# The second norm's normalised rows move from ScalarE to VectorE

## The chip, the cores and the metric

The kernel runs on one core of a Trainium2 chip. The metric is the device time of one launch in microseconds. Five engines work side by side, each through its own queue in program order: TensorE (PE in the profile), VectorE (DVE), ScalarE (ACT), GpSimd (POOL) and SyncE (SP), which issues most transfers. They wait for each other through semaphores.

## The reference

Two sequences of 1024 tokens, each of width 256, go through one adaptive-norm transformer block:

```python
h = _layernorm(x) * (1 + ca) + sa            # norm 1, modulated
# attention branch, applied to h:
x_norm = (h - mu) / sqrt(var + EPS) * gamma + beta   # norm 2
q, k, v = x_norm @ qkv ...; causal softmax; out @ o_proj; + h
x = x + ga * attention(h)
h = _layernorm(x) * (1 + cb) + sb            # norm 3
# 16 experts, top 4 of each token, and a shared expert
x = x + gb * ffn(h)
```

`sa, ca, ga, sb, cb, gb` come from a small matrix product of `silu(c)` and are the same for all tokens of a sequence. The change is inside norm 2: the rows `xn = (h - mean) / sqrt(var + EPS)` of a tile of 128 tokens, before `gamma` and `beta`.

## The kernel before

The 2048 tokens are 16 tiles of 128. The first part of the kernel, to about 160 us, is one software pipeline over steps `s` from -5 to 17. In a step every engine does a piece for several tiles, each at another stage. The order of work is written out by hand, engine by engine, in one loop per engine; nothing reorders it, so an instruction that waits holds everything behind it on its engine.

The path of tile `t` through the part that matters here:

- Step `t-5` and `t-4`, VectorE: statistics of `x_in` (L1043, L1050), `h = (x_in - mean) * (1 + ca)` (L1377). GpSimd makes `rstd = (var + EPS)^-0.5` (L594, L598). VectorE finishes `h` with `rstd` and `sa` (L1388) and takes the statistics of `h` (L1043, L1050).
- Step `t-3`, GpSimd: `inverse_std` makes norm 2's `rstd` (one operation for up to three norms of different tiles, from step 2 on), `mean_shift` makes `shift = -mean * rstd` (L604), `residual` adds the skip connection to `x1` (L613, L616). From step 9 on four scattered row transfers (L631) follow in each step.
- Step `t-3`, ScalarE: `xn = rstd * h + shift` (L868), near the end of the step.
- Step `t-2`, TensorE transposes `xn` (L1759). ScalarE applies `gamma` and `beta` and makes the high part of a split (L833, L839), VectorE the low part (L1055). Products are made as three products of high and low parts (L1540 to L1542).
- Step `t-1`, TensorE makes value and query rows (`vq`), ScalarE copies the high part (L857), VectorE the low part (L1060). Step `t`: scores, row maximum (L1356), exponential (L848). Step `t+1`: probabilities transposed (L1718), multiplied with the values, `x1` finished (L1412). Norm 3, the router and the sending of rows to the experts follow.

The start of the pipeline is mixed with preparations. On VectorE, step -3 begins with the split of a weight product (L1006), the gate `ga` of the first sequence (L982 to L991) and a gated weight product (`wvo_gate`, L1015). On TensorE the transposition of tile 0's `xn` stands ahead of the modulation of the second sequence (L1547), the modulation columns (L1599), the second gate (L1547) and the transposition of tile 1. Step 4 ends on VectorE with `wvo_gate` for the second sequence (L1015), which ScalarE splits (L719) at the start of step 5.

After the pipeline GpSimd sends the remaining rows (L631, to about 210 us), and then pairs of tiles of routed rows go through the experts (to about 325 us), and the sums are made and stored.

Of the kernel before, what the change touches and what calls it, by code (L numbers as in the profile page):

```python
# [9 lines left out]
ALU = mybir.AluOpType  # L10
ACT = mybir.ActivationFunctionType
# [9 lines left out]
TILES = B * NT  # L21
# [138 lines left out]
def place_of(n, t):  # L160


    return (t + n - 1) % 4
# [9 lines left out]
def adaln_block(nc, x, qkv, o_proj, gamma, beta, w_router, we1, we3, we2, ws1, ws3, ws2, c_in, wmod, out):  # L173
# [3 lines left out]
    with ctx:  # L177
# [10 lines left out]
        def at(name, where, shape, dt=F32):  # L188
            return nc.alloc_sbuf_tensor_at(name, list(shape), dt, offset=ORIGIN + 4 * where)

        def sb(name, shape, dt=F32):
            n = 1
            for m in shape[1:]:
                n *= m
            where = free[0]
            free[0] += (n + 7) // 8 * 8
            return at(name, where, shape, dt)
# [13 lines left out]
        h = at("h", A + 7680, [P, 2, D])  # L211
        xn = at("xn", A + 8192, [P, 2, D])
# [67 lines left out]
        mv = sb("mv", [P, 3, 4, 2])  # L280
        veps = sb("veps", [P, 3, 4])
        rstd = sb("rstd", [P, 3, 4])
        shift = sb("shift", [P, 3, 4])
# [76 lines left out]
        def pv_side(t, at_, n):  # L360
# [25 lines left out]
        tl = {n: sem("t_" + n) for n in (  # L386
            "bn1", "stat1", "u", "h", "bn2", "stat2", "xlo", "negmax", "vqlo", "ptlo", "rinv", "x1", "bn3", "stat3",
            "hlo",
            "shift2", "shift3", "rmul", "resid", "z2", "h2row", "lg",
            "xT", "vq", "scores", "pT", "h2T", "pv",  # L390
            "xn", "xf", "xhi", "exp", "vqhi", "pthi", "h2f", "hhi")}
# [3 lines left out]
        def inverted(eng, n, t):  # L395

            eng.wait_ge(s_rstd, POWERS[n, t])

        def done(eng, stage_, t):

            if t >= 0:
                eng.wait_ge(tl[stage_], t + 1)
# [143 lines left out]
        def _(pool):  # L546
# [89 lines left out]
            for s in range(FIRST, LAST + 2):  # L636
                if s < 0 <= s + 3:
                    residual(s + 3)
                for group in norms_of(s):
                    inverse_std(group)  # L640
                    for n, t in reversed(group):
                        if n > 1:
                            mean_shift(n, t)
                if 0 <= s and s + 3 < TILES:
                    residual(s + 3)
                if s == 3:
                    router_constants()
                send(SENDS.get(s, 0))
# [22 lines left out]
        def _(act):  # L671
# [8 lines left out]
            def load_table(func):  # L680

                act.wait_ge(s_eps, 1)
                if tables[0]:
# [25 lines left out]
                                 scale=D ** -0.5).then_inc(s_wqk_hi, 1)  # L709
# [82 lines left out]
            for s in range(FIRST, LAST + 1):  # L792

                if s == -2:
                    wvo_copy()
                if s == 1:
                    gate_b_copy()
                if s == 5:
                    wvo_split(1)
                if 0 <= s - 4:  # L800
                    norm2_cols(s - 4)
                if s == LAST:
                    norm2(s - 3)
                    norm2_rows(s - 5)
                t = s - 1
                if 0 <= t < TILES:

                    for u, first, n in units_of(t):
                        done(act, "pT", u)
                        if u >= PT_RING:  # L810
                            done(act, "pv", tile_of_unit(u - PT_RING))
                        nc.scalar.activation(pT_hi[:, u % PT_RING, 0:n * P], ps[:, X0 + u % 2, 0:n * P],
                                             ACT.Copy).then_inc(tl["pthi"], 1)
                if s == LAST:
                    router_exp(NG - 2)
                    load_table(ACT.Silu)
                    silu_step(0)
                if 0 <= s - 3 and s < LAST:
                    norm2(s - 3)
                if 0 <= s - 4:  # L820
                    if s - 5 >= 0 and s < LAST:
                        norm2_rows(s - 5)
                    norm2_hi(s - 4)
                t = s + 2
                if 0 <= t < TILES:

                    at = slot_of(t) * P
                    done(act, "xT", t)
                    if t == 0:
                        act.wait_ge(s_ld_cols, 32)  # L830
                    done(act, "xlo", t - 2)
                    for c in range(DC):
                        last = nc.scalar.activation(xf[:, t % 2, c, :], ps[:, Y0, c * P:(c + 1) * P], ACT.Identity,  # L833
                                                    scale=cols[:, 0, c:c + 1], bias=cols[:, 1, c:c + 1])
                    last.then_inc(tl["xf"], 1)
                    done(act, "xf", t)
                    if t >= KEY_SLOTS:
                        done(act, "scores", NT - 1)
                    nc.scalar.activation(xnT_hi[:, :, at:at + P], xf[:, t % 2, :, :], ACT.Copy  # L839
                                         ).then_inc(tl["xhi"], 1)  # L840
                t = s
                if 0 <= t < TILES:

                    done(act, "negmax", t)
                    if t >= 2:
                        done(act, "pT", units_of(t - 2)[-1][0])
                    done(act, "rinv", t - 4)
                    nc.scalar.activation(probs[:, t % 2, 0:(t % NT + 1) * P], score_banks(t), ACT.Exp,  # L848
                                         bias=negmax[:, t % 4:t % 4 + 1],
                                         accum_out=rowsum[:, t % 4:t % 4 + 1]).then_inc(tl["exp"], 1)  # L850
                t = s + 1
                if 0 <= t < TILES:
                    done(act, "vq", t)
                    done(act, "scores", t - 2)
                    if t >= KEY_SLOTS:
                        done(act, "pv", NT - 1)
                    nc.scalar.activation(vq(V_HI, Q_HI, t), ps[:, Y1, :].rearrange("p (two x) -> p two x", two=2),  # L857
                                         ACT.Copy).then_inc(tl["vqhi"], 1)
                if s == -2:
                    wvo_split(0)  # L860
                    gate_a_copy()
                    load_table(ACT.Exp)
                t = s + 3
                if 0 <= t < TILES:

                    done(act, "shift2", t)
                    done(act, "xT", t - 2)
                    nc.scalar.activation(xn[:, t % 2, :], h[:, t % 2, :], ACT.Identity,  # L868
                                         scale=rstd[:, 1, place_of(2, t):place_of(2, t) + 1], bias=shift[:, 1, t % 4:t % 4 + 1]
                                         ).then_inc(tl["xn"], 1)  # L870
                if s - 1 in RANKED_AT and s < LAST:
                    router_exp(RANKED_AT.index(s - 1))
                if 12 <= s < 12 + SH:
                    split_shared(s - 12)
# [78 lines left out]
        def _(dve):  # L953
# [91 lines left out]
            def stats_end(n, t, read_by):  # L1045
                done(dve, f"bn{n}", t)
                done(dve, read_by, t - 4)
                if n == 1 and t >= 4:
                    inverted(dve, n, t - 4)
                nc.vector.bn_aggr(mv[:, n - 1, place_of(n, t), :], bn[:, n - 1, place_of(n, t), :]).then_inc(tl[f"stat{n}"], 1)  # L1050

            def x_lo(t):
                at = slot_of(t) * P
                done(dve, "xhi", t)
                nc.vector.tensor_tensor(xnT_lo[:, :, at:at + P], xf[:, t % 2, :, :],  # L1055
                                        xnT_hi[:, :, at:at + P].bitcast(F32), ALU.subtract).then_inc(tl["xlo"], 1)
# [275 lines left out]
            for s in range(FIRST, LAST + 1):  # L1332
# [11 lines left out]
                t = s - 1  # L1344
# [7 lines left out]
                t = s  # L1352
# [7 lines left out]
                a, c = s + 5, s + 4  # L1360
# [20 lines left out]
                    stats_end(1, a, "u")  # L1381
                if 0 <= s + 2 < TILES and s > -1:
                    x_lo(s + 2)
                if 0 <= c < TILES:

                    inverted(dve, 1, c)
                    done(dve, "u", c)
                    nc.vector.scalar_tensor_tensor(out=h[:, c % 2, :], in0=h[:, c % 2, :],  # L1388
                                                   scalar=rstd[:, 0, c % 4:c % 4 + 1], in1=mod_a[:, c // NT, 0:D],
                                                   op0=ALU.mult, op1=ALU.add).then_inc(tl["h"], 1)  # L1390
                t = s - 1
# [10 lines left out]
                t = s - 1  # L1402
# [10 lines left out]
                                                   scalar=rinv[:, t % 4:t % 4 + 1], in1=x1[:, t, :],  # L1413
                                                   op0=ALU.mult, op1=ALU.add).then_inc(tl["x1"], 1)
                if 0 <= c < TILES:
                    stats_end(2, c, "shift2")
                if 0 <= t < TILES:
                    done(dve, "x1", t)
                    stats(3, x1[:, t, :], t)
# [546 lines left out]
```

## Time and profile before

| | |
|---|---|
| Times of three runs | 377.86, 380.18, 382.19 us |
| Median | 380.18 us |
| Profiled execution, span from first to last instruction | 380.9 us |
| TensorE busy | 329.5 us, 87% of the span |
| VectorE busy | 258.2 us, 68% |
| GpSimd busy | 213.2 us, 56% |
| ScalarE busy | 197.8 us, 52% |
| Mean granted TensorE clock | 0.952 of full |

The profiled execution has no time of its own in the record beside its span of 380.9 us, which is 0.7 us above the median of the three runs. In rows of the timeline the first number is the start in us from the span's start, the second how long the instruction or the merged run of instructions took. Square brackets give the idle time of the engine ahead of the row and who ended it. Instructions of one engine overlap by a little under 0.1 us, so the distance from start to start is shorter than the time of one.

### The profile page before, as it was taken

Reading aid. Unit: us, or ns where it says so; the run is one execution under the profiler, and the core shown is the slowest. Engines: PE = TensorE matmul, PEld = TensorE weight load, DVE = VectorE, ACT = ScalarE, POOL = GpSimd, SP = SyncE. Lnnn points to the kernel's source line nnn. Section 1 sums busy time; section 2 is a strip of 40 time slices with the busy share of each in tenths; the row PEclk is TensorE's granted clock in tenths of the full one; section 3 lists DMA queues with packets and bytes.
Section 4 is the critical chain, followed back from the end, with each engine's and each line's share of the span. In section 5 each row is a group of like instructions: output and inputs, shape, how many; then the busy total and the mean of one; then the engine's idle time right before and its main releaser. Section 6 shows DMA issues by size and latency. Waiting matters only on the chain.

```text
span 380.9 us, 8085 instructions
## 1 busy us (share of the span) xinstructions
PE 329.5 (87%) x2296; PEld 305.0 (80%) x2296; DVE 258.2 (68%) x720; ACT 197.8 (52%) x436; POOL 213.2 (56%) x289
## 2 busy tenths in 40 slices
PE   3986997997888999999890399999999998999890
PEld 1676997997887899898770389999999998988770
DVE  1888895578985886757891379656656555516996
ACT  2456666465675656746340078656666665621100
POOL 1486563333388887757777007766666666651240
PEclk9999897799999999999997589999999999999997
DMA  6346500000011229982232346666675666239952
GB/s 217 115 148 203 166 28 16 8 20 14 3 62 70 79 92 316 305 271 111 108 126 108 95 98 183 186 184 201 174 207 166 197 187 175 91 91 412 409 191 83
DMA packets 54554, 56.36 MB, mean 148 GB/s; under 512 B 17424, under 2 KB 46864, under 8 KB 54512
## 3 DMA queue, kind: packets, MB, share of 16 engines
q1 hardware_dynamic: 46560, 34.21, 30.6%
q0 software_dynamic: 6864, 19.80, 13.7%
q10 hardware_dynamic: 1088, 1.84, 1.4%
q8 instruction: 21, 0.34, 0.4%
q14 instruction: 21, 0.17, 0.2%
HBM read 31.43 MB, written 24.40 MB: 147 GB/s over the span
## 4 chain that ended last, share of the span: by engine, by line
PE 44%; POOL 13%; DVE 11%; DMA 10%; issue 9%; SPq 8%; ACT 3%; DVEq 0%; POOLq 0%; ACTq 0%
PE ps L1540 11%; PE ps L1541 11%; PE ps L1542 11%; POOL xg_rows L631 7%; DMA y_in<-y_rows 4%; SPq L523 3%; PE ps L1863 3%; SPq L518 3%; POOL y_rows L658 2%; DMA x_in<-in_L_attn_x_dram 2%; DMA xs<-xg_rows 2%; PE ps L1694 1%; PE ps L1896 1%; POOL rstd L598 1%; PE ps L1633 1%
## 5 line engine op out<-in xcount | busy, mean ns | idle before, releaser
L658 POOL DMA_INDIRECT y_rows<-y_sb,aside x79 | 76.5, 969 | 53.0 <-ACT y_sb L930 38.9
L631 POOL DMA_INDIRECT xg_rows<-hrow,slot_u x64 | 66.3, 1037 | 20.7 <-issue 18.9
L1540 PE MATMUL ps<-rpool 128*128 128x256 f32 (+3 forms) x228 | 70.8, 311 | 6.3 <-DVE rpool L1060 6.2
L1541 PE MATMUL ps<-rpool 128*128 128x256 f32 (+3 forms) x228 | 67.8, 297 | 0.0
L1542 PE MATMUL ps<-rpool 128*128 128x256 f32 (+3 forms) x228 | 67.7, 297 | 0.0
L1540 PEld LDWEIGHTS ps<-rpool 128*128 128x128 f32 x228 | 45.5, 200 | 8.9 <-DVE rpool L1060 8.3
L1540 PE MATMUL ps<-w_hi_routed,xT_hi 128*128 x158 | 45.8, 290 | 2.2 <-DVE xT_lo L1469 2.1
L1542 PEld LDWEIGHTS ps<-rpool 128*128 128x128 f32 x228 | 45.5, 199 | 0.6
L1541 PEld LDWEIGHTS ps<-rpool 128*128 128x128 f32 x228 | 45.5, 200 | 0.5
L1542 PE MATMUL ps<-w_hi_routed,xT_lo 128*128 x158 | 45.2, 286 | 0.0
L1541 PE MATMUL ps<-w_lo_routed,xT_hi 128*128 x158 | 45.2, 286 | 0.0
L1469 DVE TENSOR_TENSOR xT_lo<-ps,xT_hi 128x512 fp32r<-128x512 f32 x40 | 27.6, 691 | 17.1 <-ACT xT_hi L905 17.1
L1863 PE MATMUL ps<-ident,xs 128*128 128x128 f32 x158 | 25.0, 284 | 15.1 <-DMA xs<-xg_rows 15.1
L594 POOL TENSOR_TENSOR veps<-mv,eps 128x1 f32<-128x1 f32 (+2 forms) x26 | 6.7, 257 | 53.6 <-DVE mv L1050 53.2
L905 ACT ACTIVATE xT_hi<-ps 128x512 fp32r<-128x512 f32 x40 | 24.0, 599 | 21.2 <-PE ps L1863 19.4
L1540 PEld LDWEIGHTS ps<-w_hi_routed,xT_hi 128*128 128x128 f32 x158 | 30.7, 194 | 3.4 <-issue 3.4
L1487 DVE TENSOR_TENSOR aside<-ends,aside 128x2 int32<-128x2 int32 (+1 forms) x40 | 6.5, 162 | 39.4 <-ACT r_silu L921 39.4
L921 ACT ACTIVATE r_silu<-ps 128x256 f32<-128x256 f32 x40 | 15.4, 385 | 33.6 <-PE ps L1542 30.9
L1863 PEld LDWEIGHTS ps<-ident,xs 128*128 128x128 f32 x158 | 19.2, 146 | 15.7 <-DMA xs<-xg_rows 15.7
L1542 PEld LDWEIGHTS ps<-w_hi_routed,xT_lo 128*128 128x128 f32 x158 | 30.8, 195 | 0.0
L1541 PEld LDWEIGHTS ps<-w_lo_routed,xT_hi 128*128 128x128 f32 x158 | 30.8, 195 | 0.0
L1540 PE MATMUL ps<-h2T_hi,w_hi_shared 128*128 128x512 f32 x64 | 26.9, 420 | 0.0
(208 smaller groups left out, 893.4 us busy)
## 6 DMA issues: line engine op xcount, KB each, us to landing
xs<-xg_rows SPq DMA_DIRECT2D x79, 128.0 KB
y_in<-y_rows SPq DMA_DIRECT2D x8, 1024.0 KB, 12.1
xg_rows<-empty SPq DMA_DIRECT2D x1, 2304.0 KB, 8.2
x_in<-in_L_attn_x_dram SPq DMA_DIRECT2D x16, 128.0 KB, 2.1
w_raw_routed<-in_L_ffn_we_dram SPq DMA_DIRECT2D x8, 256.0 KB, 3.8
out_dram<-x SPq DMA_DIRECT2D x16, 128.0 KB, 2.4
wmod_sb<-in_L_wmod_dram ACTq DMA_DIRECT2D x3, 512.0 KB, 7.4
w_raw_routed<-in_L_ffn_we_dram SPq DMA_DIRECT2D x4, 320.0 KB, 7.0
```

The source lines that it names most:

```text
L518: sp.dma_start(xs[:, r, i, :], xg[bass.ds(row[i], P), 0:D]).then_inc(s_xs[r], 16)
L523: sp.dma_start(ends[:, r, i, :], xg[bass.ds(row[i], P), bass.ds(col[i], 2)]).then_inc(s_ends[r], 16)
L594: nc.gpsimd.tensor_tensor(v, mv[:, norms, j, 1], eps[:].broadcast_to(wide), ALU.add).then_inc(s_veps, 1)
L631: nc.gpsimd.indirect_dma_start(out=xg, out_offset=bass.IndirectOffsetOnAxis(ap=slot_u[:, t, k:k + 1].bitcast(U32), axis=0), in_=hrow[:, t, ...
L658: nc.gpsimd.indirect_dma_start(out=yb, out_offset=bass.IndirectOffsetOnAxis(ap=dest[:, 2 * n + i:2 * n + i + 1].bitcast(U32), axis=0), in_ ...
L905: nc.scalar.activation(xT_hi[:, n % 2].rearrange("p i c t -> p (i c t)"), ps[:, 6 + n % 2, :], ACT.Copy).then_inc(s_rxhi, 1)
L921: nc.scalar.activation(r_silu[:, n % 2], ps[:, n % 2, :].rearrange("p (i w) -> p i w", i=2)[:, :, 0:H], ACT.Silu).then_inc(s_rsilu, 1)
L1469: nc.vector.tensor_tensor(xT_lo[:, n % 2].rearrange("p i c t -> p (i c t)"), ps[:, 6 + n % 2, :], xT_hi[:, n % 2].rearrange("p i c t -> p ...
L1540: nc.tensor.matmul(dst, w[0], x_[0], start=first, stop=False)
L1541: nc.tensor.matmul(dst, w[0], x_[1], start=False, stop=False)
L1542: return nc.tensor.matmul(dst, w[1], x_[0], start=False, stop=last)
L1863: last = nc.tensor.transpose(ps[:, 6 + n % 2, (i * DC + c) * P:(i * DC + c + 1) * P], xs[:, n % RING, i, c * P:(c + 1) * P], ident[:])
```

## The change

ScalarE's activation for `xn` and GpSimd's `shift` of norm 2 go. VectorE makes `xn` in one operation, `(h - mean) * rstd`, with mean and `rstd` read per partition. It stands in the step of before (`t-3`), between the low part of tile `s+2` and the second half of `h` of tile `s+4`, and waits for `rstd` of norm 2, for VectorE's own statistics and for the transposition of tile `t-2`. The statistics of `h` four tiles on now wait for `xn`, which is on the same engine. Norm 3 keeps its shift on GpSimd and its activation on ScalarE.

```diff
@@ GpSimd
                     inverse_std(group)
-                    for n, t in reversed(group):
-                        if n > 1:
+                    for n, t in group:
+                        if n == 3:
                             mean_shift(n, t)
@@ ScalarE
-                t = s + 3
-                if 0 <= t < TILES:
-
-                    done(act, "shift2", t)
-                    done(act, "xT", t - 2)
-                    nc.scalar.activation(xn[:, t % 2, :], h[:, t % 2, :], ACT.Identity,
-                                         scale=rstd[:, 1, place_of(2, t):place_of(2, t) + 1], bias=shift[:, 1, t % 4:t % 4 + 1]
-                                         ).then_inc(tl["xn"], 1)
@@ VectorE
                 if 0 <= s + 2 < TILES and s > -1:
                     x_lo(s + 2)
+                t = s + 3
+                if 0 <= t < TILES:
+
+                    j = place_of(2, t)
+                    inverted(dve, 2, t)
+                    done(dve, "stat2", t)
+                    done(dve, "xT", t - 2)
+                    nc.vector.tensor_scalar(xn[:, t % 2, :], h[:, t % 2, :], mv[:, 1, j, 0:1], rstd[:, 1, j:j + 1],
+                                            ALU.subtract, ALU.mult).then_inc(tl["xn"], 1)
                 if 0 <= c < TILES:
@@ VectorE, statistics of h
-                    stats_end(2, c, "shift2")
+                    stats_end(2, c, "xn")
```

Where the new operation falls for tile 0 is seen on VectorE in step -3. Before, the engine's row reads as follows (`gate_tmp` and `mod_a` are the gate, `wT_sb` the gated weight product, `mv` a mean and variance):

```order
L1006 SCALAR_TENSOR_TENSOR rpool<-ps,rpool 128x512
L982 TENSOR_SCALAR gate_tmp<-ps 128x256
L984 COPY mod_a<-ps 128x256
L986 SCALAR_TENSOR_TENSOR mod_a<-mod_a 128x256
L989 TENSOR_SCALAR mod_a<-mod_a 128x256
L991 SCALAR_TENSOR_TENSOR mod_a<-gate_tmp,mod_a 128x256
L1015 TENSOR_TENSOR wT_sb<-wT_sb,mod_a 128x256 x2
L1043 BN_STATS bn<-x_in 128x6
L1377 SCALAR_TENSOR_TENSOR h<-x_in,mv,mod_a 128x256
L1050 BN_AGGR mv<-bn 128x2
L1388 SCALAR_TENSOR_TENSOR h<-h,rstd,mod_a 128x256
```

With the change the same place on VectorE reads (L1383 is the new operation; the other lines are those above, eight lower, and L1389 the old L1388):

```order
L998 SCALAR_TENSOR_TENSOR rpool<-ps,rpool 128x512
L974 TENSOR_SCALAR gate_tmp<-ps 128x256
L976 COPY mod_a<-ps 128x256
L978 SCALAR_TENSOR_TENSOR mod_a<-mod_a 128x256
L981 TENSOR_SCALAR mod_a<-mod_a 128x256
L983 SCALAR_TENSOR_TENSOR mod_a<-gate_tmp,mod_a 128x256
L1007 TENSOR_TENSOR wT_sb<-wT_sb,mod_a 128x256 x2
L1035 BN_STATS bn<-x_in 128x6
L1369 SCALAR_TENSOR_TENSOR h<-x_in,mv,mod_a 128x256
L1042 BN_AGGR mv<-bn 128x2
L1383 TENSOR_SCALAR xn<-h,mv,rstd 128x256
L1389 SCALAR_TENSOR_TENSOR h<-h,rstd,mod_a 128x256
```

Tile 0's `xn` now stands behind the weight split, the gate, the gated weight product and the first half of tile 1's `h`.

On ScalarE it stood ahead of the copy of the weight product (L714), as this piece of the difference shows:

```order
 L704 ACTIVATE wT_sb<-ps 128x512
 L708 ACTIVATE rpool<-ps 128x512
-L868 ACTIVATE xn<-h,shift,rstd 128x256
 L714 ACTIVATE wT_sb<-ps 128x512
 L833 ACTIVATE xf<-ps,cols 128x128 x2
```

Nothing stood ahead of it there but the copies of the weight products, so it ran as soon as `shift` was there. TensorE's order is unchanged.

## Rows read from the trace of the kernel before

**Rows 1.** The page's chain of work that ended last, by engine.

```profile
PE 44%; POOL 13%; DVE 11%; DMA 10%; issue 9%; SPq 8%; ACT 3%; DVEq 0%; POOLq 0%; ACTq 0%
```

**Rows 2.** Windows: stretch, length, then busy time per engine, PEclk, DMA share, GB/s.

```profile
36.00:40.00 4.00, 2.86 (x11) 2.86 (x12) 3.34 (x12) 0.46 (x3) 1.17 (x3) 0.67 0.80 226
40.00:44.00 4.00, 3.68 (x28) 3.44 (x27) 3.21 (x9) 3.29 (x9) 2.09 (x4) 0.90 0.82 235
...
60.00:64.00 4.00, 2.90 (x15) 2.93 (x16) 3.46 (x9) 3.36 (x10) 0.93 (x2) 0.66 0.13 37
64.00:68.00 4.00, 4.00 (x20) 4.00 (x20) 1.03 (x2) 1.08 (x2) 0.00 (x0) 0.50 0.01 2
68.00:72.00 4.00, 4.00 (x21) 3.92 (x20) 2.14 (x8) 1.53 (x4) 0.72 (x2) 0.56 0.00 0
...
120.00:124.00 4.00, 3.38 (x28) 3.31 (x29) 3.84 (x19) 3.40 (x9) 3.45 (x6) 1.00 0.09 36
```

**Rows 3.** Timeline of TensorE, 14 to 38 us.

```profile
14.37 1.89 PE L1578 MATMUL ps<-o_sb,wT_sb 128*128 128x256 f32 x8
16.69 0.44 PE L1759 MATMUL ps<-ident,xn 128*128 128x128 f32 x2 [0.42 <-ACT xn L868]
16.96 2.75 PE L1547 MATMUL ps<-wmod_sb,silu_b 128*128 128x512 f32 x8
...
21.25 1.11 PE L1547 MATMUL ps<-wmod_sb,silu_b 128*128 128x256 f32 x4
23.14 0.44 PE L1759 MATMUL ps<-ident,xn 128*128 128x128 f32 x2 [0.78 <-ACT xn L868]
...
37.14 0.53 PE L1540 MATMUL ps<-rpool 128*128 128x384 f32 x1 [1.60 <-DVE rpool L1060]
```

**Rows 4.** Timeline of VectorE, 18 to 35 us.

```profile
18.88 0.61 DVE L1377 SCALAR_TENSOR_TENSOR h<-x_in,mv,mod_a 128x256 f32<-128x256 f32 x1
19.41 0.17 DVE L1050 BATCH_NORM_AGGREGATE mv<-bn 128x2 f32<-128x6 f32 x1
...
26.85 1.03 DVE L1377 SCALAR_TENSOR_TENSOR h<-x_in,mv,mod_a 128x256 f32<-128x256 f32 x1
...
34.82 0.43 DVE L1043 BATCH_NORM_STATS2 bn<-x_in 128x6 f32<-128x256 f32 x1 [1.51 <-DMA x_in<-in_L_attn_x_dram]
```

**Rows 5.** Instructions of a line: count, then ns shortest/median/longest, first and last start.

```profile
L868 ACT ACTIVATE xn<-h,shift,rstd x16: 589/598/601, 16.0 to 128.7; 128x256 f32<-128x256 f32 x16
...
L604 POOL TENSOR_SCALAR shift<-mv,rstd x32: 261/267/740, 15.7 to 166.3; 128x1 f32<-128x1 f32 x32
...
L989 DVE TENSOR_SCALAR mod_a<-mod_a x2: 293/295/297, 16.5 to 51.1; 128x256 f32<-128x256 f32 x2
...
L1377 DVE SCALAR_TENSOR_TENSOR h<-x_in,mv,mod_a x16: 466/468/1031, 13.0 to 114.2; 128x256 f32<-128x256 f32 x16
...
L1388 DVE SCALAR_TENSOR_TENSOR h<-h,rstd,mod_a x16: 472/482/953, 13.6 to 119.4; 128x256 f32<-128x256 f32 x16
```

**Rows 6.** Groups by line on VectorE, 188 to 193 us: busy us, mean ns.

```profile
L1204 DVE TENSOR_SCALAR tb<-tb,lane 128x16 f32<-128x16 f32 x1 | 0.2, 227 | 0.0
...
L1199 DVE TENSOR_SCALAR tb<-tb 128x16 f32<-128x16 f32 x1 | 0.2, 174 | 0.0
```

**Rows 7.** Timeline of TensorE: the waits in steps 5 and 11.

```profile
61.10 0.54 PE L1759 MATMUL ps<-ident,xn 128*128 128x128 f32 x2 [2.23 <-ACT hrow L790]
...
120.62 0.38 PE L1540 MATMUL ps<-rpool 128*128 128x256 f32 x1 [1.86 <-DVE rpool L1060]
```

**Rows 8.** Timeline of GpSimd, steps 9 to 11.

```profile
101.78 0.51 POOL L604 TENSOR_SCALAR shift<-mv,rstd 128x1 f32<-128x1 f32 x2
...
110.51 0.79 POOL L604 TENSOR_SCALAR shift<-mv,rstd 128x1 f32<-128x1 f32 x2
...
118.49 0.89 POOL L598 TENSOR_TENSOR rstd<-veps,minus_half 128x3 f32<-128x3 f32 x1
```

**Rows 9.** Timeline of VectorE, step 11.

```profile
119.42 0.48 DVE L1388 SCALAR_TENSOR_TENSOR h<-h,rstd,mod_a 128x256 f32<-128x256 f32 x1 [3.34 <-POOL rstd L598]
```

## The prediction

> **What bounds the kernel now.** I read the chain that ended last first: TensorE has 44% of it, GpSimd 13%, VectorE 11%, ScalarE 3% [rows 1]. So the engine that is relieved most carries almost nothing of the end, and ScalarE's 16 activations of 0.598 us, 9.6 us of busy time [rows 5], say little about the time. Then I went through the timelines of the pipeline, since the change lies in it alone, and asked in each step who waits last. From step 12 on TensorE has no idle time worth naming, and the sending of rows and the experts start from its end, so what the steps up to there win or lose moves everything behind them by the same amount. Four places are not TensorE's own: the start up to 44 us, where VectorE, GpSimd and a transfer take turns; step 4 to 5, where TensorE sits idle for 2.23 us behind a chain that starts on VectorE [rows 7]; steps 9 to 11, where GpSimd is full and VectorE waits 3.34 us for its `rstd` [rows 9]; and two spells at half clock. Those show in the windows: from 36 to 44 us the granted clock is 0.67 and 0.90, from 60 to 72 us it is 0.66, 0.50, 0.56 [rows 2]. Lost clock is 4 x (0.33 + 0.10) = 1.7 us in the first and 4 x (0.34 + 0.50 + 0.44) = 5.1 us in the second. Both begin when TensorE comes back from a wait, of 1.60 us [rows 3] and of 2.23 us [rows 7]. A wait of 1.86 us at 120.62 did not lower it: 120 to 124 us is at 1.00 [rows 2, 7].
>
> **The price of the new operation.** No row shows it. Nearest is the one-input operation on 128x256 numbers from SBUF with constants, 0.295 us; from start to start it is some 0.08 less [rows 5]. A scalar read per partition costs 0.227 - 0.174 = 0.05 us in a small operation [rows 6]. With two of them I take 0.40 us, 0.3 from start to start, because shape and memory are those of the first row. The lower bound is 0.22, the upper 0.95 - 0.08 = 0.87, the longest `h` operation beside GpSimd [rows 5]. It comes 16 times, 6.4 us of busy time; what counts is the places where nothing covers it.
>
> A rule speaks against the move. The trace shows the same two-input operation at 0.468 us and once at 1.03 us, at 26.85, while GpSimd adds tiles [rows 4, 5]. The Trainium skill, page "GPSIMD Engine Reference", section "8. Key points", says that GpSimd shares its SBUF interfaces with VectorE, and that they contend when VectorE runs in a mode that uses two ports or reads two SBUF inputs; "VectorE: DVE Perf Modes", section "Mode 2×_2P", says that a fp32 operation with one tensor input and scalars runs in such a mode. By that each new operation would contend too, which is the third rival below.
>
> **Start, tile 0.** This is the largest term. Before, ScalarE made tile 0's `xn` at 16.03 and TensorE transposed it at 16.69 after only 0.42 us idle [rows 3, 5]. Now the operation stands on VectorE behind the gate and the first half of tile 1's `h`, which ends its statistics at 19.41 + 0.17 = 19.58 [rows 4]. With 0.40 us that gives 20.0: TensorE starts the transposition 3.3 us later and is idle from 16.26 (14.37 + 1.89) to 20.0, 3.7 us. Queued behind it on TensorE are the second sequence's modulation, its columns and the second gate, from 16.96 to 22.36, which don't need `xn` at all. They end at 20.27 + 5.4 = 25.67. Tile 1's transposition was at 23.14 after 0.78 us idle [rows 3], so of the 3.3 us 2.5 stay. Tile 1's own `xn` (VectorE, about 23.5) is in time.
>
> From there the delay runs through value rows, ScalarE's copy and VectorE. VectorE's 26.85 becomes 29.35. From 26.85 to 34.82 it idled 1.51 us for a tile of `x` [rows 4] and was nearly full otherwise, so it has 6.46 us of work. Two new operations add 0.6; the 0.56 us that the 1.03 us operation lost beside GpSimd goes, since GpSimd's additions for that step are done by then. 29.35 + 6.46 + 0.6 - 0.56 = 35.85 against 34.82: the transfer is no longer what ends the wait, and 1.0 us is lost. A third new operation comes before the row that TensorE waits for at 37.14: 1.0 + 0.3 = **+1.3 us** there (+1.1 to +1.9 by the bounds of the price).
>
> But TensorE's wait ahead of 37.14 nearly closes, because its own work before it is 2.5 us later and VectorE's only 1.3: 1.60 - 1.2 = 0.4 us. Then the half-clock spell that follows should not come. It cost 1.7 us; VectorE, which has one more operation in step 2, takes a part of that back, and I count **-1.2 us** (0 to -1.7).
>
> **The clock after the new wait.** 3.7 us idle at 16.26 is longer than both waits after which the clock fell. What TensorE does after it, 5.4 us of modulation and then the value rows, is all on the path. If a spell comes there, it costs like the shorter one, **+1.7 us**, with 0 and 5.1 (the longer one) as ends. I take the short one since the long one has only one instance in two.
>
> **Steps 2 to 8.** The shift of norm 2 on GpSimd and the activation on ScalarE leave, and neither is waited for last. In steps 2, 3 and 5 to 8 VectorE has idle time in each step that covers 0.3 us. Step 4 has none: VectorE runs through to the weight product after which ScalarE, and then TensorE at 61.10, go on [rows 7]. **+0.3 us** (0.2 to 0.9); the 2.23 us wait becomes 2.5, and the long spell after it stays.
>
> **Steps 9 to 11.** GpSimd's steps follow each other without a gap. Its pair of shifts takes 0.51 and 0.79 us [rows 8]; one of 0.267 goes from each, and the second pair is stretched by VectorE's operation beside it, so 0.25 to 0.5 each: `rstd` of step 11 comes at 119.38 - 0.6. On VectorE `xn` now comes ahead of `h` there, +0.3. So the row at 119.42, and TensorE's 120.62 and the router's work behind it, gain **-0.3 us** (0 to -0.6; with the price at its upper bound it is +0.3). VectorE's `h` can only be released by that `rstd`, so this is all that the shift's removal is worth. In step 12 ScalarE loses the activation from a chain that TensorE waits 0.15 us for: **-0.15**. Steps 13 on have no `xn`.
>
> **Sum.** +1.3 - 1.2 + 1.7 + 0.3 - 0.3 - 0.15 = +1.65 us, on the span of 380.9: 382.55. The median of the three runs is 0.7 lower: **381.9 us**. I expect a change of +0.4%, less than can be measured well: the three runs lie 4.3 us apart, and about 1% is what a measurement of this kernel tells from no change.
>
> **Rivals.**
> 1. The clock does not fall after the new wait. For: TensorE's wait at 120.62 passed without [rows 7]. Against: it is twice as long now. The 1.7 goes: 380.2.
> 2. Slower: the clock falls there and stays low as long as from 61 to 72 us. That is 5.1 in place of 1.7, 3.4 more, 385.3. It decides as soon as the low stretch covers the value rows of tiles 0 to 2. For: it happened after the 2.23 us wait. Against: TensorE's first work is dense there, as in the shorter spell.
> 3. Slower: the new operation stalls beside GpSimd. `rstd` releases `xn` and GpSimd's additions at the same moment, so they run together. The price by row is 1.03 - 0.47 = 0.56 us on each of the five that lie on the path: +2.5 after rounding down for those that miss, 384.4.
> 4. Faster: the spell of 60 to 72 us does not come, because its wait starts at another moment. VectorE and ScalarE are mostly idle there, so 3.5 to 5.1 of it come back: about 4.3, 377.6. For: ScalarE is free earlier. Against: the wait starts on VectorE, which has more to do.
> 5. That the change does nothing but shift busy time (tile 0's `xn` is not later because TensorE had been held by something else). The row at 16.69 names `xn` as what ended the wait [rows 3]; it would give 380, as rival 1.
>
> **How the numbers follow.** The forecast has 0.45 (its own range 380.3 to 383.6), rivals 1 and 5 together 0.20, rival 2 0.13, rival 3 0.08, rival 4 0.14. The range of 377.4 to 385.6 leaves out the far half of rivals 2 and 4, about 0.15. Faster by over 1% is below 376.4: the better part of rival 4's tail and a gain I do not see, 0.09. Slower by over 1% is above 384.0: rivals 2 and 3, less what falls short, 0.20. Within 1%: 0.71.
>
> **What the profile of the changed kernel would show.** TensorE's transposition of tile 0 at about 20.0, with 3.7 us idle before it, released by VectorE; tile 1's at 25 to 26, or later at half clock. Granted clock under 1 somewhere between 19 and 28 us, and 1.00 from 37 to 41. No wait of VectorE for the transfer at 35. `xn` at about 0.4 us on VectorE; over 0.8 in many of the 16 speaks for rival 3. GpSimd's three `rstd` at 110 and 118 earlier by 0.3 to 0.6 against the tile before. I am wrong if tile 0's transposition is not late, if VectorE still waits for the transfer at 35, or if the low spell at 61 us is missing or doubled.

## The result: 1.8% slower, outside the range

| | median, us | runs |
|---|---|---|
| before | 380.14 | 4, from 377.86 to 382.19 |
| with the change | 387.44 | 4, from 385.76 to 388.74 |

The ratio is 1.018, with a 95% interval of 1.012 to 1.023. Measured again later on another chip, beside experiments, it was 1.017 (1.013 to 1.022). The forecast was 381.9 us, at most 385.6.

The profiled execution of the changed kernel took 385.76 us with a span of 384.0, so some 1.8 us lie around the span, as in all its runs. If the same holds for before, its profiled span of 380.9 us is an execution of 382.7 us, 2.5 above its median, while the profile of the change is the fastest of its four runs. The two spans therefore differ by only 3.1 us where the medians differ by 7.3. Keep this in mind with every comparison of two traces here.

Medians below are over all runs of a kernel, while the ratios leave out the slowest executions, over 1.5% above the kernel's fastest, so the two can differ (shift kept, and tiles 7 to 15 with the hold, where half the runs or more lie that high).

**The profile after.** The page's chain of work that ended last, by engine:

```profile
PE 40%; DVE 18%; issue 12%; POOL 11%; DMA 8%; SPq 7%; ACT 2%; DVEq 0%; POOLq 0%; ACTq 0%
```

VectorE went from 11% to 18% and TensorE from 44% to 40% [rows 1]: there are more places now where VectorE is what the rest waits for. TensorE's timeline, 13 to 70 us, the rows with over 0.7 us of idle time ahead of them:

```profile
19.37 0.69 PE L1760 MATMUL ps<-ident,xn 128*128 128x128 f32 x2 [3.65 <-DVE xn L1383]
...
35.66 0.39 PE L1541 MATMUL ps<-rpool 128*128 128x256 f32 x1 [2.04 <-DVE rpool L1052]
41.90 0.45 PE L1541 MATMUL ps<-rpool 128*128 128x384 f32 x1 [0.79 <-DVE rpool L1052]
47.65 0.50 PE L1541 MATMUL ps<-rpool 128*128 128x512 f32 x1 [1.06 <-DVE rpool L1052]
...
65.68 0.41 PE L1760 MATMUL ps<-ident,xn 128*128 128x128 f32 x2 [2.20 <-ACT hrow L790]
```

The first row is the forecast one (20.0 with 3.7 us idle), the last the wait of step 5 that [rows 7] shows before. The other three are step 0, step 1 and step 2 waiting for VectorE's value rows; before, the waits of over 0.7 us up to step 3 were 0.78 us at 23.14 and 1.60 us at 37.14 [rows 3], and 1.28 us at 31.64. Windows of the changed kernel, columns as in [rows 2]:

```profile
16.00:20.00 4.00, 0.63 (x3) 0.63 (x4) 3.83 (x10) 0.35 (x1) 2.58 (x4) 0.90 0.06 20
20.00:24.00 4.00, 4.00 (x12) 2.09 (x10) 3.28 (x8) 1.75 (x5) 2.38 (x6) 0.68 0.08 23
...
36.00:40.00 4.00, 4.00 (x25) 4.00 (x23) 3.56 (x12) 1.68 (x5) 2.40 (x4) 0.57 0.12 30
...
64.00:68.00 4.00, 2.32 (x17) 2.35 (x17) 3.14 (x8) 3.68 (x10) 1.26 (x2) 0.87 0.11 37
68.00:72.00 4.00, 4.00 (x20) 4.00 (x20) 1.66 (x5) 0.87 (x3) 0.00 (x0) 0.50 0.00 0
72.00:76.00 4.00, 4.00 (x23) 3.74 (x23) 2.71 (x9) 1.99 (x6) 1.06 (x2) 0.78 0.00 0
```

Half clock is a granted clock of 0.50, 1.2 GHz in place of 2.4. Lost clock: 4 x (0.10 + 0.32) = 1.7 us after the new wait, 4 x 0.43 = 1.7 us at 36, 4 x (0.13 + 0.50 + 0.22) = 3.4 us at 64. Before it was 0, 1.7 and 5.1.

**Where VectorE lost time.** Step 0 on VectorE and beside it on GpSimd:

```profile
32.94 0.39 DVE L1047 TENSOR_TENSOR rpool<-xf,rpool 128x256 fp32r<-128x256 f32 x1
33.25 0.82 DVE L1383 TENSOR_SCALAR xn<-h,mv,rstd 128x256 f32<-128x256 f32 x1
33.99 1.01 DVE L1389 SCALAR_TENSOR_TENSOR h<-h,rstd,mod_a 128x256 f32<-128x256 f32 x1
34.92 0.68 DVE L1052 TENSOR_TENSOR rpool<-ps,rpool 128x512 fp32r<-128x512 f32 x1
```

```profile
32.91 1.01 POOL L613 TENSOR_TENSOR x<-h,mod_a 128x256 f32<-128x256 f32 x1
33.99 0.72 POOL L616 TENSOR_TENSOR x<-x,x_in 128x256 f32<-128x256 f32 x1
```

`xn` takes 0.82 us beside L613 and `h` 1.01 us beside L616, where alone they take 0.41 and 0.48. L1052 is what TensorE's row at 35.66 waits for. The pair comes again in step 2 (0.83 at 45.17, 1.01 at 45.92), and step 3 has L1047 at 1.01 and `xn` at 0.82. GpSimd's L613 is stretched too, to 1.01 us from 0.73, beside VectorE's L1047. Over all lone VectorE instructions from 12 to 60 us, what they took beyond their undisturbed time is 4.1 us. About 1.0 of it lies in step -2 (L1047 at 21.38, 0.88 us, and L1013 at 22.18, 1.21 in place of 0.68) and has idle time of VectorE behind it. In the trace of before the sum is 2.1 us: L1377 at 26.85 [rows 4], the two below, and two more.

```profile
22.50 0.91 DVE L1388 SCALAR_TENSOR_TENSOR h<-h,rstd,mod_a 128x256 f32<-128x256 f32 x1
...
41.49 0.95 DVE L1388 SCALAR_TENSOR_TENSOR h<-h,rstd,mod_a 128x256 f32<-128x256 f32 x1
```

### The profile page after: what moved, and what is told of

Its sections match the earlier page's. It is cut to its first block, busy times and chain, and to the rows that moved or that the text cites. A ratio compares the mean times of both kernels' runs of the same rounds, so it can differ in the third digit from the quotient of the medians.

```text
span 384.0 us, 8071 instructions
## 1 busy us (share of the span) xinstructions
PE 329.3 (86%) x2296; PEld 304.0 (79%) x2296; DVE 265.3 (69%) x736; ACT 189.4 (49%) x420; POOL 207.4 (54%) x273
## 4 chain that ended last, share of the span: by engine, by line
PE 40%; DVE 18%; issue 12%; POOL 11%; DMA 8%; SPq 7%; ACT 2%; DVEq 0%; POOLq 0%; ACTq 0%
PE ps L1541 10%; PE ps L1542 9%; PE ps L1543 9%; POOL xg_rows L631 7%; DMA y_in<-y_rows 4%; PE ps L1864 3%; SPq L518 3%; PE ps L1548 2%; SPq L523 2%; POOL y_rows L658 2%; DVE bn L1035 2%; DMA xs<-xg_rows 2%; PE ps L1695 1%; PE ps L1897 1%; DMA cols<-in_L_c_dram 1%
## 5 line engine op out<-in xcount | busy, mean ns | idle before, releaser
L658 POOL DMA_INDIRECT y_rows<-y_sb,aside x79 | 76.4, 967 | 53.4 <-ACT y_sb L922 39.3
L631 POOL DMA_INDIRECT xg_rows<-hrow,slot_u x64 | 64.9, 1014 | 20.6 <-issue 18.9
L594 POOL TENSOR_TENSOR veps<-mv,eps 128x1 f32<-128x1 f32 (+2 forms) x26 | 5.9, 228 | 62.1 <-DVE mv L1042 61.9
```

The costliest lines, as they stand in the source:

```text
L631: nc.gpsimd.indirect_dma_start(out=xg, out_offset=bass.IndirectOffsetOnAxis(ap=slot_u[:, t, k:k + 1].bitcast(U32), axis=0), in_=hrow[:, t, ...
L658: nc.gpsimd.indirect_dma_start(out=yb, out_offset=bass.IndirectOffsetOnAxis(ap=dest[:, 2 * n + i:2 * n + i + 1].bitcast(U32), axis=0), in_ ...
```

## The experiments

**How they are read.** Half-clock stretches differ from execution to execution, so I give, beside the times, one distance inside each trace: from VectorE's second half of `h` in step -3 to TensorE's transposition of `xn` in step 5 (61.10 in [rows 7]). It leaves out how late the first load came. "Clock" is what was lost at half clock between 12 and 60 us, and then between 60 and 80 us, summed from windows of 4 us. "Rest" is the distance less the first. It is a help and not exact, since a lower clock also hides in waits: two traces of one and the same kernel (before with the hold, below) have a rest of 37.9 and 39.6 us.

| kernel | median (before beside it), us | ratio, 95% | distance | clock | rest |
|---|---|---|---|---|---|
| before | | | 41.5 | 1.7, 5.1 | 39.8 |
| change | 387.4 (380.1) | 1.018 (1.012 to 1.023) | 46.5 | 3.4, 3.4 | 43.1 |
| tile 0 early | 386.4 (380.7) | 1.014 (1.010 to 1.019) | 44.1 | 3.4, 3.4 | 40.7 |
| tile 0 on ScalarE | 384.5 (380.7) | 1.009 (1.005 to 1.013) | 44.0 | 3.4, 3.4 | 40.6 |
| only tile 0 on VectorE | 380.9 (380.7) | 1.000 (0.997 to 1.003) | 41.4 | 0, 3.4 | 41.4 |
| before and an extra operation | 383.3 (380.7) | 1.009 (1.005 to 1.012) | 43.1 | 3.4, 0 | 39.7 |
| change, shift kept | 387.5 (380.3) | 1.009 (1.005 to 1.014) | 46.6 | 5.1, 3.4 | 41.5 |
| tiles 12 to 15 | 381.3 (380.3) | 1.001 (0.996 to 1.005) | 40.7 | 1.7, 0 | 39.0 |
| tiles 7 to 15 | 381.8 (380.3) | 0.998 (0.995 to 1.002) | 41.7 | 1.7, 5.1 | 40.0 |
| change and hold | 379.6 (380.3) | 0.995 (0.992 to 0.999) | 42.8 | 1.7, 0 | 41.1 |

The control runs on a slower chip, where before takes 419 to 420 us, follow further down.

### Tile 0 placed early on VectorE

```diff
 wqk_split()
+normalised(0)        # the new operation, for tile 0
 gate_a(0)
...
-if 0 <= t < TILES:
+if 0 < t < TILES:
```

> The change, with tile 0's xn on VectorE placed earlier: right after the split of the weight product and ahead of the gate and of tile 1's h. Tiles 1 to 15 stay where the change has them. Theory A (the late tile 0 is most of the loss: TensorE waits 3.65 us for it, and the half-clock stretch from 19 to 24 us follows that wait): TensorE's transposition comes back to under 18.0, the clock from 16 to 24 us is 1.0, and 3 to 4.5 of the 7.3 us come back: 383 to 384.5. Theory B (what counts is the operation itself in the steps 0 to 5, where it and h run beside GpSimd's additions at 0.8 to 1.0 us each): nothing of that changes, 386 to 388. The plain time of the operation (0.3 us in each of the six steps to step 3, rival C) also leaves 386 to 388.

Measured: 386.4 us, ratio 1.014. Tile 0's `xn` is at 16.61 and TensorE's first wait is gone, but the half-clock stretch is not: it now follows a wait of 2.61 us for tile 1's `xn`, at 25.36. Theory A fails in size: 1.0 us came back by the two medians, 1.3 by the ratios, not 3 to 4.5.

### Tile 0 on ScalarE, the others on VectorE

> Tile 0 as before the change (GpSimd's shift, ScalarE's activation), tiles 1 to 15 as in the change. Theory A: TensorE's transposition of tile 0 at about 16.7, no half-clock stretch before 30 us, 382.5 to 384. It should be within 1 us of the kernel with tile 0 early on VectorE; if it is faster by more, VectorE's time in step -3 counts by itself. Theory B: 386 to 388 still.

Measured: 384.5 us, ratio 1.009, between the two theories' ranges. Half of the loss, some 3.4 us, stays without anything late at tile 0. It is 1.9 us faster than tile 0 early on VectorE, so what VectorE does in step -3 counts too. VectorE from 43 us on still reads 0.83 (`xn`) and 1.01 (`h`). Against theory A there is still half clock before 30 us: it begins at 24 us, behind a wait of only 1.30 us for tile 1's `xn`, and costs 3.4 us with what follows up to 32 us. That `xn` took 0.71 us and the `h` ahead of it 0.94, both beside GpSimd's additions.

### Only tile 0 on VectorE

> The reverse: only tile 0 on VectorE, at the change's place; tiles 1 to 15 as before, on ScalarE with GpSimd's shift. Theory A: TensorE waits 3.7 us for tile 0, the clock falls from 18 to 24 us, and 3 to 4.5 us are lost against before: 383 to 384.5. Theory B: the other 15 operations carry the loss, 380 to 381.5.

Measured: 380.9 us, ratio 1.000. This is what the forecast had described for the start. TensorE's row and two windows:

```profile
20.84 0.44 PE L1776 MATMUL ps<-ident,xn 128*128 128x128 f32 x2 [3.66 <-DVE xn L1083]
```

```profile
20.00:24.00 4.00, 3.16 (x14) 2.10 (x14) 3.40 (x9) 1.85 (x5) 2.87 (x8) 1.00 0.10 33
36.00:40.00 4.00, 3.05 (x27) 2.81 (x26) 3.87 (x11) 3.04 (x8) 2.53 (x4) 1.00 0.18 45
```

The wait of 3.66 us is there in full, the clock does not fall after it, and the stretch at 36 us does not come either. The distance is 41.4 against 41.5 of before: 1.6 us of work lost (rest 41.4 against 39.8), 1.7 us of clock won. Theory A falls: the late tile 0 alone costs nothing that can be measured. With the other fifteen tiles on VectorE too it costs some 3 us (387.4 against the 384.5 of the experiment above). That the slack which takes it up here is filled there is my reading; no run shows it.

### Before, and the new operation beside it

```diff
+nc.vector.tensor_scalar(extra[:, t % 2, :], h[:, t % 2, :], mv[:, 1, j, 0:1], rstd[:, 1, j:j + 1],
+                        ALU.subtract, ALU.mult)      # where the change has xn; nothing reads it
```

> The kernel before, which still uses ScalarE's xn, with the new VectorE operation added at the change's place, its output into memory that nothing reads. It leaves nothing out; it measures the operation's time on VectorE alone. Theory A: only the operation's own time counts, 0.3 us in the places that nothing covers: 380.5 to 382. Theory B: the operations of steps 0, 2 and 3 that lie beside GpSimd's additions show 0.8 us as in the change, and 383 to 385 results. If they show 0.4 us here, GpSimd's shift, which is still there, keeps the additions away from them, and a time under 382 then says that it was the removed shift that brought the collision.

Measured: 383.3 us, ratio 1.009, theory B's number, though only half of what the change costs. The first pair of collisions is in step -2 here, with GpSimd's shift still in place. VectorE and GpSimd:

```profile
22.80 0.87 DVE L1394 TENSOR_SCALAR extra<-h,mv,rstd 128x256 f32<-128x256 f32 x1
23.60 1.02 DVE L1400 SCALAR_TENSOR_TENSOR h<-h,rstd,mod_a 128x256 f32<-128x256 f32 x1
```

```profile
22.81 0.72 POOL L615 TENSOR_TENSOR x<-h,mod_a 128x256 f32<-128x256 f32 x1
23.61 0.73 POOL L618 TENSOR_TENSOR x<-x,x_in 128x256 f32<-128x256 f32 x1
```

In this one trace the stalls from 12 to 60 us are 4.0 us, but the rest is no longer than that of before; the distance is longer by the clock (3.4 us lost, not 1.7). So the trace alone does not explain the time.

### The change with GpSimd's shift kept

```diff
-for n, t in group:
-    if n == 3:
+for n, t in reversed(group):
+    if n > 1:
         mean_shift(n, t)
```

> The change, but GpSimd still makes norm 2's shift, which nothing uses then (only the statistics four tiles on wait for it, as before). So GpSimd's additions start some 0.26 us after rstd as before, not at once. Theory B in its stronger form (it is the removed shift that brings the collision): xn mostly at 0.41 us in steps 0 to 3, 384 to 386. Without it: xn and h stall all the same, or the time stays, 387 to 388; steps 9 to 11 lose 0.3 us again in either case, by my fifth step.

Measured: median 387.5 us, as slow as the change, but a ratio of 1.009 (1.005 to 1.014), half its loss. Its twelve runs lie between 382.8 and 390.6 us, so this does not settle how much of the loss stays. The trace is clearer. Other operations stall (`h` 0.94 us in step 0, `xn` 0.81 in step 1 and 0.83 in step 2), 3.9 us in all: the operation on VectorE runs into the additions with the shift in place too. Whether the missing shift adds to the loss is open, since both kernels that keep all shifts and have the new operation, this and the one before it, are at 1.009 against 1.018.

### Only late tiles on VectorE: 12 to 15, and 7 to 15

> Only tiles 12 to 15, whose xn falls in steps 9 to 12, go to VectorE and lose their shift on GpSimd; tiles 0 to 11 are as before. By step five of the prediction this gains 0.3 to 0.45 us: 379.5 to 380.5 where before is 380.1. Theories B and C agree here, since VectorE has idle time in these steps; more than 382 would contradict both.

> Tiles 7 to 15 (steps 4 to 12) go to VectorE, tiles 0 to 6 are as before. If the loss lies in the steps up to 3, as both theories have it, this is at most 0.3 us slower (step 4) less the 0.3 to 0.45 of steps 9 to 12: 379.5 to 381.5. If it is over 383, the loss comes from the later steps, through the half-clock stretch behind step 5's wait.

Measured: 381.3 and 381.8 us, ratios 1.001 and 0.998, the medians a little above both expected ranges. Within the 0.5% that the intervals leave, the whole loss comes from the new operations up to step 3. A gain of 0.3 us by the GpSimd steps is too small to be seen in these times.

### The change with a hold on GpSimd's additions

```diff
 if 0 <= s and s + 3 < TILES:
+    if s < 9:
+        done(pool, "h", s + 4)      # wait until VectorE has made h of tile s+4
     residual(s + 3)
```

> The change, and in steps 0 to 8 GpSimd's additions (L613, L616) wait until VectorE has made h of tile s+4, so that neither xn nor the second half of h can lie beside them. In the change three xn took 0.82 us instead of 0.41 and two halves of h 1.01 instead of 0.47, some 2.3 us in steps 0 to 3. Theory B (contention with GpSimd is the cost of tiles 1 to 15): all xn and h at 0.41 and 0.47 in these steps, and 2 to 3 us come back, 384.5 to 385.5. Theory C (the plain time of the operation, 0.3 us in each step in which VectorE has no idle time, and what the slipped steps do to the half-clock stretches): the stalls move to the operations behind h, or go without the time coming back: 386.5 to 388.

Measured: 379.6 us, ratio 0.995 (0.992 to 0.999): 8 us faster than the change by the medians, and not slower than before. Theory B had foreseen only 2 to 3 us of that. VectorE in step 0, which in the change read 0.82 and 1.01, and GpSimd's addition, which now comes behind it:

```profile
34.59 0.41 DVE L1075 TENSOR_SCALAR xn<-h,mv,rstd 128x256 f32<-128x256 f32 x1
34.91 0.48 DVE L1397 SCALAR_TENSOR_TENSOR h<-h,rstd,mod_a 128x256 f32<-128x256 f32 x1
```

```profile
35.47 0.73 POOL L614 TENSOR_TENSOR x<-h,mod_a 128x256 f32<-128x256 f32 x1 [1.20 <-DVE h L1397]
```

All 16 `xn`, and the two stretches of the clock:

```profile
L1075 DVE TENSOR_SCALAR xn<-h,mv,rstd x16: 374/406/413, 20.1 to 123.8; 128x256 f32<-128x256 f32 x16
```

```profile
36.00:40.00 4.00, 3.76 (x32) 3.67 (x32) 3.83 (x14) 2.23 (x7) 1.80 (x4) 1.00 0.10 33
...
64.00:68.00 4.00, 4.00 (x37) 4.00 (x37) 3.03 (x10) 2.25 (x6) 1.47 (x2) 1.00 0.02 4
68.00:72.00 4.00, 4.00 (x29) 3.75 (x28) 3.39 (x10) 2.88 (x8) 1.59 (x3) 1.00 0.10 33
```

The longest `xn` is 0.413 us (in the change 0.827), and the stalls up to 60 us fall from 4.1 to 1.0 us, all that is left of them before 25 us. TensorE's first wait of the change is still there (3.66 us at 20.57) with its half-clock stretch after it. The stall time itself is less than half of the 8 us; the stretches at 36 and 64 us don't come, which gives another 1.7 and 3.4 us in this trace. It has a later one that the change has not (116 to 120 us, 1.7 us), and gives back 2 us more while the experts run (6.6 us ahead of the change at VectorE's first `xT_lo` of the experts, 212.1 against 218.7, and 4.6 at the last, 325.6 against 330.2), so of the 8 us of the medians the two spans show 4.7.

### Is the hold a gain of its own?

The same two added lines in the kernel before; the change with the hold and tile 0 on ScalarE; and with the hold and tiles 7 to 15 on VectorE only.

> The control: the kernel before with the same hold on GpSimd's additions in steps 0 to 8, xn still on ScalarE. The change with the hold took 379.6 us, 0.5% under before. If the hold only takes away what the change brought (theory B), it has little to give here, since before shows just two stalled halves of h (0.91 us in step -2, which the hold does not reach, and 0.95 us in step 2): 379.7 to 380.5. If the hold is a gain of its own of several us, which theory B would not need, this comes out at 374 to 377 and the change still costs 3 to 5 us beside it.

> The change with the hold, and tile 0 on ScalarE as before, so that TensorE does not wait 3.7 us for it. If tile 0's place costs something once the contention is gone, this is faster than 379.6 by up to 2 us: 377.5 to 379. If the slack of the steps after it takes it up, as it did with tile 0 alone on VectorE (380.9 against 380.7), the same 379 to 380.

> The hold, tiles 0 to 6 on ScalarE as before, tiles 7 to 15 on VectorE. No new operation lies in the steps up to 3, so nothing can be lost there; GpSimd's shifts are gone in steps 9 to 11. If the plain time of the operation counts in steps -3 to 3, this is the fastest of the three, by 0.3 us a step or some 1 to 2 us: 377 to 379. If not, it is at 379 to 380.5 like the others.

These ran on a chip where before itself takes 419.2 us. The medians are 416.9, 415.0 and 416.7, the ratios 0.998 (0.994 to 1.002), 0.992 (0.988 to 0.996) and 0.987 (0.983 to 0.992); the last is out of line with its own median, which is 0.6% under before. Since they can't be set beside 379.6 us, four were run side by side on the same chip:

> The change itself again, beside the three others on one chip. 1.3 to 2.3% over before, as first measured (1.8%).

> The change with GpSimd's additions held behind h in steps 0 to 8, again. Theory B: 0.0 to 0.8% under before, and 1.5 to 2.5% under the change.

> Before with the same hold. If the change's cost was contention alone, this is within 0.4% of the change with the hold. If the operation's plain time counts beside it (VectorE was 1.8 us later at step 5 with the change and the hold than with the hold alone, in the traces of the other chip), this is 0.5 to 1% faster than the change with the hold.

> The change with the hold and tile 0 on ScalarE. If the late tile 0 costs nothing once the stalls are gone, within 0.3% of the change with the hold; if it costs the 1 us that its step -2 to 3 show, 0.3 to 0.6% faster.

And twice more on a chip of the first kind:

> The hold with tiles 7 to 15 on VectorE, tiles 0 to 6 on ScalarE. The traces so far have VectorE 0.7 to 1.1 us earlier than before at steps 4 and 5, and GpSimd 0.8 us quicker through steps 8 to 11: 0.4 to 0.7% under before, not the 1.3% of its first measurement.

> The change with the hold, all tiles on VectorE, a third time: the two measurements so far are 0.5% under and 0.2% over before. Within 0.4% of before; 0.3 to 0.7% slower than the kernel beside it, if the operation's plain time in the early steps counts.

| side by side | median, us | ratio, 95% | distance | clock | rest |
|---|---|---|---|---|---|
| first measurement, before | 419.2 | 1 | | | |
| before, hold | 416.9 | 0.998 (0.994 to 1.002) | 41.3 | 3.4, 5.1 | 37.9 |
| change, hold, tile 0 on ScalarE | 415.0 | 0.992 (0.988 to 0.996) | 42.7 | 3.4, 0 | 39.3 |
| hold, tiles 7 to 15 | 416.7 | 0.987 (0.983 to 0.992) | 39.8 | 0, 0 | 39.8 |
| second measurement, before | 420.0 | 1 | | | |
| change | 426.1 | 1.017 (1.013 to 1.022) | 47.4 | 5.1, 3.4 | 42.3 |
| change, hold | 419.8 | 1.002 (0.996 to 1.008) | 42.8 | 1.7, 0 | 41.1 |
| before, hold | 417.5 | 0.994 (0.988 to 1.000) | 39.6 | 0, 0 | 39.6 |
| change, hold, tile 0 on ScalarE | 419.0 | 0.997 (0.991 to 1.002) | 39.5 | 0, 0 | 39.5 |
| first kind of chip, before | 381.5 | 1 | | | |
| change, hold | 381.0 | 0.998 (0.995 to 1.001) | 42.8 | 1.7, 0 | 41.1 |
| hold, tiles 7 to 15 | 381.4 | 0.995 (0.991 to 1.000) | 41.3 | 1.7, 5.1 | 39.6 |

The tables show this. The hold takes the change from 1.8% over before to between 0.5% under and 0.2% over it, in three measurements. Before with the hold is at 0.998 and 0.994, so the hold may be worth 0.2 to 0.6% by itself, against the 1.5 to 2.3% that it gives the change. So the like comparison, change with hold against before with hold, leaves the change up to 0.8% slower (1.002 against 0.994 side by side, with intervals that overlap), where it is 1.7% without: the hold takes back the larger part, and part of what it gives would have been there for before as well. Last, the traces leave it open whether fifteen `xn` on VectorE still cost something with the additions out of the way and tile 0 on ScalarE. The second measurement says no (39.5 against 39.6 us up to step 5, both with no half clock), the first says 1.4 us (42.7 against 41.3, both with 3.4 us of it), and the times say no. The rest of 41.1 in all three traces of the change with the hold is 1.6 above the 39.5 with tile 0 on ScalarE, as much as was seen with only tile 0 on VectorE.

No version is clearly faster than before: the two lowest ratios, 0.987 and 0.992, came back as 0.995 and 0.997 when the kernels were measured again. The hold with tiles 7 to 15 is then 0.5% under before with an interval that just reaches 1.000, and its median is 0.1 us under that of before.

## Why the prediction was wrong

The forecast summed a late tile 0, clock and plain operation time. The experiments show another cause, the one it had as rival 3.

**The failing step: the price of the new operation was taken without company.** Undisturbed it was right, 0.41 us against 0.40 taken, and 0.33 from start to start. But the sum took this price for every place and put contention with GpSimd's additions at nothing, with rival 3 at 0.08. Three of the 16 `xn` took 0.82 to 0.83 us, and two halves of `h` went to 1.01 us, because the new operation pushed them under the second addition; the rival had priced only the new operation. It gave 384.4 against 387.4, and it also let the clock alone. Its premise holds only in part: one `rstd` lets both start, but VectorE stood waiting for `rstd` before only two of the 16 `xn`. They meet where VectorE happens to arrive during the additions. The cause of the larger part is shown: with the additions moved and nothing else, 8 us are gone (6.2 us side by side), while keeping the shift, moving tile 0, or taking it away leaves a half or more.

The rows of before already bore it: `h` at 1.03 us at 26.85, and `h` up to 0.953 in [rows 4, 5]. I had used the first as a credit (0.56 us that goes) and not asked where the shifted operations land. The rule of the Trainium skill that the prediction cited holds here: an operation with one tensor input and scalars stalls beside GpSimd's (0.82 us in place of 0.41). The Trainium skill, page "SBUF — State Buffer", section "🔬 SBUF: two separate sides", goes further: the shared ports are locked for a whole instruction by whoever starts first, and the other waits. The traces agree on the whole instruction: in step 0 GpSimd's L613 begins at 32.91 and ends at 33.92, and `xn`, begun at 33.25, ends 0.15 us behind it, at 34.07; `h`, begun at 33.99, ends 0.29 us behind L616. They do not bear out who wins by the recorded starts: in the trace with the extra operation that operation starts 0.01 us ahead of the addition and is the one that stalls, and the `h` at 26.85 of before starts 0.02 us ahead.

**The start, tile 0: right.** 3.65 us idle at 19.37 (forecast 3.7 at 20.0). In isolation the +1.3 measured as 1.6, and the -1.2 for the stretch at 36 us as 1.7, net 0 in the time. In the change the -1.2 failed: TensorE's wait there did not shrink to 0.4 but was 2.04 us at 35.66, since the two stalls lie right ahead of the L1052 that it waits for. The stretch came, 1.7 us. VectorE no longer waited for the transfer at 35 us, as forecast.

**The clock after the new wait: right.** +1.7 forecast, 1.7 measured; that the size fits so well is luck, since the forecast borrowed it from another stretch and gave it 0 to 5.1. In all six traces with every `xn` in the change's place the wait of 3.65 us is followed by about 1.7 us of lost clock. With only tile 0 on VectorE the same wait left the clock at 1.00, so the wait alone does not decide it.

**Steps 4 to 8.** The +0.3 of step 4 can't be told apart, nor can the -0.15 of step 12. The long stretch was 3.4 us, not 5.1.

**Steps 9 to 11: a size.** From `h` in step 8 to `h` in step 11 the change took 21.7 us (100.37 to 122.05) against 22.5 (96.97 to 119.42 [rows 9]): 0.8 us gained, 0.3 forecast. VectorE waits 3.01 us for `rstd` there (3.34 before). One trace each, so this is a hint at the size and no more.

**The sum.** By step 5 it was +1.3 - 1.2 + 1.7 + 0.3 = +2.1; the distance grew by 5.0. The difference of 2.9 is 1.2 us for the stretch that did not go away and, as an estimate from what is left, 1.7 us of stalls and what they move. The 0.7 us between span and median set a span against a whole execution, but it cancels: what was forecast is a change of 1.65 us on either.

**What stays open.** The medians differ by 7.3 us and the traces show 5.0 by step 5, less 0.4 for an earlier start, and 1.5 us of that given back by the end. Single traces carry 1.7 to 5.1 us of half clock that other executions of the same kernel have elsewhere, so the split of the rest between stalls and clock is not settled. The stalls add up to 2 us more than before, so most of the 7.3 us is what they move and the clock that follows, which no run takes apart. Nor is it shown why the kernel before gained so little from losing its own stalls, whether the missing shift has a part, or why the experts give back some of the lead.

## What to carry to other kernels

When an operation goes to an engine that shares something with another, price it beside what that other engine does at the same moment, and look at what slides into that moment behind it. Here both follow the same `rstd`, so they meet whenever VectorE comes to its rows within the 1.5 us of the two additions. Moving the other engine's work behind it, with one wait, took back most of what the move had cost. Give the same wait to the kernel before as well: what it gains there is not the change's. A step that is late alone, with slack behind it, can be free and cost several microseconds once something fills the slack: test a change's parts both alone and taken out.

## What the runs showed of the hardware

- **A stalled operation ends a fixed time behind GpSimd's instruction, so the stall has no fixed price.** In the 19 traces up to 140 us, counting what ran over 0.2 us too long, all 85 two-input operations on 128x256 (`h` and the low parts L1047/L1055) end 0.27 to 0.29 us behind the addition they were caught by, and 17 of 19 `xn` 0.14 to 0.16 us behind it. So the stall is the longer the earlier in the addition the operation comes: 0.65 to 1.05 us in all. The other two `xn` are where memory fills follow the addition at once; in the second trace of the change, at 53.49, it took 1.33 us:

```profile
53.49 1.33 DVE L1383 TENSOR_SCALAR xn<-h,mv,rstd 128x256 f32<-128x256 f32 x1
54.74 0.47 DVE L1389 SCALAR_TENSOR_TENSOR h<-h,rstd,mod_a 128x256 f32<-128x256 f32 x1
```

```profile
53.36 0.80 POOL L616 TENSOR_TENSOR x<-x,x_in 128x256 f32<-128x256 f32 x1
54.11 0.20 POOL L563 MEMSET ones<- 128x128 f32 x1
```

  In the first trace the fill is the one that waits: `xn` at 51.85 ends after 0.82 us, and L563 takes 0.35.

- **The length of a wait did not tell whether the clock falls after it.** TensorE's wait in step 5 was followed by half clock after 1.93 us (before with the hold, first trace), 2.05, 2.23 and 2.43 us, and by none after 1.93 us (the same kernel, second trace), 2.11, 2.23 and 2.43 us.
- **Chips differ by 10%.** The same kernel took 380 us on one chip and 419 us on another. Up to step 5 the traces of the change with the hold agree (42.8 us on both). The experts take most of the difference: from the first to the last `xT_lo` the change took 111.5 us on one chip (218.7 to 330.2) and 141.5 on the other (226.8 to 368.3).
